# An attention pass whose VectorE turn is put in another order: products before differences, totals before the cap

## The reference, cut to what matters

```python
Q = _ln(h @ Wq[i], gq[i], bq[i])
K = _ln(h @ Wk[i], gk[i], bk[i])
qi = Q[src]
kj = K[dst]
score = (qi * kj).sum(-1) + 0.1 * (edge_attr * qi[:, :RBF]).sum(-1) + logm[dst]
smax = jax.ops.segment_max(score, src, num_segments=N)
es = jnp.exp(jnp.minimum(score - smax[src], 20.0))
denom = jax.ops.segment_sum(es, src, num_segments=N)
alpha = es / (denom[src] + 1e-10)
m = h[dst] @ Wm[i]
aggi = jax.ops.segment_sum(alpha[:, None] * m, src, num_segments=N)
```

## Time and profile before

| | |
|---|---|
| median of 3 runs | 11525.92 us (11525.92 to 11526.84) |
| the profiled execution | 11507.11 us, span 11505.3 us |
| busy in the span | PE 8060.2, PEld 6419.3, DVE 6381.7, ACT 3299.7, POOL 4649.4 us |
| the four attention passes | from 4787.25 to about 8521 us of the span, with tables and updates between them |
| `top` (L1648) | 1488 times, 683 ns each in the middle |
| `keys`, `products`, `totals` | 1488 times each, 358, 351 and 356 ns |
| `differences`, `capped` | 1488 times each, 158 and 156 ns |

### The profile page before, as it was taken

One profiled execution on the slowest core, in us unless ns is written; L12 is line 12 of the kernel. 1 busy time (PEld: TensorE's weight loads), 2 busy tenths in 40 slices (PEclk: granted clock), 3 DMA queues, 4 the chain that ended last, 5 costly groups with the idle time before them and its releaser, 6 DMA issues. The chain is left out here.

```text
span 11505.3 us, 328287 instructions
## 1 busy us (share of the span) xinstructions
PE 8060.2 (70%) x107650; PEld 6419.3 (56%) x107651; DVE 6381.7 (55%) x21371; ACT 3299.7 (29%) x11512; POOL 4649.4 (40%) x6184
## 2 busy tenths in 40 slices
PE   2999943234777588499599769949967889962323
PEld 1777732223555477499489659938963444443323
DVE  6444453335999767688678958868872010011112
ACT  3222211112333233266256536626640000010000
POOL 0777767775000166255145415514530000026665
PEclk9999985555767699799699879969988999955555
DMA  7222223334777699399279649928957889801112
GB/s 293 59 59 59 59 59 79 72 81 120 222 223 222 179 292 311 101 248 248 71 215 248 177 111 248 248 60 226 247 141 294 356 343 372 354 24 18 18 18 18
DMA packets 2228522, 1954.48 MB, mean 170 GB/s; under 512 B 1472897, under 2 KB 1871505, under 8 KB 2189698
## 3 DMA queue, kind: packets, MB, share of 16 engines
q1 hardware_dynamic: 1872642, 1712.86, 48.6%
q10 hardware_dynamic: 252000, 173.83, 4.9%
q0 software_dynamic: 103712, 65.58, 3.8%
HBM read 1478.99 MB, written 470.93 MB: 169 GB/s over the span
## 5 line engine op out<-in xcount | busy, mean ns | idle before, releaser
L1615 POOL TENSOR_TENSOR s_rest<-s_msg 128x196 f32<-128x196 f32 x1488 | 764.3, 514 | 2232.9 <-ACT s_msg L1597 1821.5
L2104 POOL DMA_INDIRECT l_row<-H,l_rec x816 | 786.9, 964 | 2158.9 <-DMA l_rec<-REC 1839.1
L1214 PE MATMUL s_gotd<-m_table_d,s_hot 128*128 x17856 | 1423.5, 205 | 201.1 <-DMA s_hot<-OHT 193.4
L1597 ACT ACTIVATE s_msg<-s_gotd,s_es 128x49 f32<-128x49 f32 x5952 | 1310.0, 304 | 48.7 <-ACT s_es L1590 0.5
L1214 PE MATMUL s_small<-m_table_s,s_hot 128*128 x17856 | 1301.6, 185 | 0.7 <-issue 0.2
L1214 PEld LDWEIGHTS s_gotd<-m_table_d,s_hot 128*128 128x128 bf16 x17856 | 1030.8, 96 | 399.0 <-issue 233.4
L846 DVE SCALAR_TENSOR_TENSOR a_acc<-a_acc,m_keep,a_sums 128x256 f32<-128x256 f32 x1488 | 707.2, 475 | 807.8 <-remote 751.6
L455 POOL DMA_INDIRECT REC<-rec,place x800 | 949.8, 1187 | 322.7 <-issue 215.1
L746 POOL DMA_INDIRECT REC<-m_meta,m_place x800 | 951.0, 1189 | 294.9 <-issue 243.6
L791 PE MATMUL a_ptr<-m_ident_bf,a_hd 128*128 128x128 bf16 x1488 | 295.0, 275 | 1094.3 <-DVE a_hd_weighted L832 756.0
L1648 DVE TENSOR_REDUCE s_tops<-s_mt 128x512 f32 (+1 forms) x1488 | 1014.7, 682 | 2.0 <-PE s_mt L1558 1.7
(11 more groups left out here) (414 smaller groups left out, 19900.6 us busy)
## 6 DMA issues: line engine op xcount, KB each, us to landing
s_hot<-OHT SPq DMA_DIRECT2D x1488, 384.0 KB
p_row<-ADJ SPq DMA_DIRECT2D x288, 1600.0 KB
ADJ<-a_acc SPq DMA_DIRECT2D x1488, 128.0 KB
s_rec<-REC SPq DMA_DIRECT2D x1488, 98.0 KB
OHT<-a_turned ACTq DMA_DIRECT2D x372, 384.0 KB
g_hot<-OHT SPq DMA_DIRECT2D x372, 384.0 KB
REC<-fill SPq DMA_DIRECT2D x124, 624.0 KB, 10.2
g_rec<-REC SPq DMA_DIRECT2D x372, 108.0 KB
```

The source lines that it names most:

```text
L1214: last = nc.tensor.matmul(out, hot, table[k][:, bass.ds(at, w)], start=(k == 0), stop=(k == 2))
L1597: last = nc.scalar.activation(msg[:, b % KEPT, j], gotd[b % KEPT][:, j, SW:2 * SW], ACT.Copy, scale=es[:, b % 2, j:j + 1])
L1615: nc.gpsimd.tensor_tensor(rest[:, b % KEPT].rearrange("p g w -> p (g w)"), msg[:, b % KEPT].rearrange("p g w -> p (g w)"), upper(msg[:, b ...
L2104: nc.gpsimd.indirect_dma_start(out=row[:, b, j], out_offset=None, in_=table, in_offset=bass.IndirectOffsetOnAxis(ap=rec[:, b, j, GIDX - NO ...
```

## The change

The list that orders VectorE's six stages in a turn is permuted; the stages, their lags, waits and increments stay the same.

```diff
-                laps(dve, [(keys, 1), (differences, 3), (products, 1), (capped, 3), (totals, 1), (top, 2)],
+                laps(dve, [(keys, 1), (products, 1), (differences, 3), (totals, 1), (capped, 3), (top, 2)],
                      SLOTS)
```

## The result

| | before | after |
|---|---|---|
| median, same chip | 11526.38 us (4 runs, 11525.92 to 11538.57) | 11600.47 us (4 runs, 11589.44 to 11619.53) |
| ratio | | 1.0063, interval 1.0046 to 1.0081 |
| the profiled execution | 11507.11 us | 11589.44 us, span 11587.6 us |
| four passes, first keys to last keys | 769.7, 769.9, 771.2, 772.0 us | 788.6, 788.8, 786.5, 788.6 us |
| a round of twelve turns, median | 23.90 us | 24.49 us |

The change makes the kernel slower by 74 us, 0.6%. The forecast was 11525 and its range ended at 11575. In the profiled executions 82 us came on; the four passes hold 69.7 of them between their first and last keys, and 116 rounds x 0.59 = 68 us of that. The rest had come on before the first pass (its first keys start at 4800.96 us of the span instead of 4787.25), in code that is the same.

A forecast was written before the change was run, and what follows sets the result against it. TensorE's own list, some 1.92 us a turn, was taken to bound the kernel. Floor cost 9 us minus branch gain 10 gave 11506 on the profiled 11507.1, plus 19 for timed runs: 11525; eight-in-ten range 11508 to 11575.

The forecast's parts named there:

- TensorE sets the regular turn at 1.92, neither wait holds it: Attention loop: TensorE works through its own list, some 1.92 us a turn, not held by its waits for differences or maximum.
- Products 0.39 behind keys, differences ending at 0.82: VectorE's regular turn: products move from 0.53 to 0.39 behind the keys' start, differences from 0.45 to 0.66, ending at 0.82.
- The order closes a loop that is a floor: Gathers' end, keys, products, differences, next gathers: a floor of 1.92 us a turn, costing 0.08 a round, 9 us.
- I take 0.05, being the row in which the wait itself is last.: Price of TensorE's wait for the differences at the gathers, 0.05 us, taken from a weight load in the adjacency pass.
- the bound of 0.13: Turn behind the branch: 0.13 us from differences' end to gathers holds the whole wait, so the floor is at most 2.00.
- the dearer wait: Rival, chance 0.14: the wait at the gathers costs more than 0.05; 11555 at a floor of 1.95, some 11604 at 2.00.
- The gain behind the branch: Turn behind the loop's branch: earlier maximum from totals ahead of the cap, turn from 2.01 to 1.92, 10 us gained.
- The caught cap: Rival, chance 0.16: the cap waits up to 0.37 for GpSimd's second subtraction; one hit a round 11546, three 11588.
- The prediction's 0.37: Turn behind the branch: the cap got through 0.37 us after the start of GpSimd's subtraction, of 0.51 recorded.
- No floor: Rival, chance 0.13: products start 0.27 behind keys like an unrelated neighbour, only a gain of 17 us remains, 11509.

The follow-up runs named there:

- Experiment 5: Kernel before, order unchanged, gathered maxima put in free columns of their own group's bank, gathers no longer wait for the differences; 10575.85 us against 10615.88, ratio 0.9965.
- experiment 1: Kernel before with only the products moved, directly behind the keys; cap still ahead of totals; 11495.52 us against 11406.79 for the kernel before, ratio 1.0086.
- experiment 6: Changed kernel with only the gathers' wait for the loaded data moved ahead of TensorE's address work; 10698.76 us against 10615.88 for the kernel before, ratio 1.0081.
- experiment 7: Changed kernel with the same three waits on the first gather, the differences' listed first; 10618.5 us against 10615.88 for the kernel before, ratio 1.0004.
- experiment 8: Changed kernel with the cap taken against a number in the instruction instead of a constant tile; 10689.78 us against 10615.88 for the kernel before, ratio 1.0072.
- Experiment 3: Changed kernel with gathered maxima in free columns of their group's bank, no gathers' wait for the differences; 11337.67 us against 11406.79 for the kernel before, ratio 0.994.
- experiment 4: Changed kernel with the gathers' waits for data and messages moved ahead of TensorE's address work; 11626.29 us against 11406.79 for the kernel before, ratio 1.0187.
- experiment 2: Kernel before with only the totals moved ahead of the cap; 11429.82 us against 11406.79 for the kernel before, ratio 1.0016.

## Why the prediction was wrong, step by step

- *TensorE sets the regular turn at 1.92, neither wait holds it.* Right. Experiment 5 takes the wait for the differences away in the old order and the rounds stay at 23.9.
- *Products 0.39 behind keys, differences ending at 0.82.* Right, 0.39 to 0.40 and 0.82. The view that gave it was one pair in another part of the pass.
- *The order closes a loop that is a floor.* Right, and it is what costs: in the changed kernel and in experiments 1, 6, 7 and 8 the regular turn is 0.82 (keys' start to differences' end) + the wait + 1.05, to within 0.01: 1.99 with a wait of 0.12 and 1.92 with one of 0.05. Experiment 3, without the wait, has the own pace again.
- ***"I take 0.05, being the row in which the wait itself is last."*** This step failed. The wait measured 0.11 to 0.12 in all regular turns looked at. The floor is 1.99, not 1.92, and a loop that stood exactly at TensorE's pace stands 0.07 above it: ten turns a round, 116 rounds. The earlier trace rows is a weight load that carries its one wait itself; the gathers' first load carries the first of three, and the differences' wait, the last, stands on an extra instruction ahead of it (experiment 7). That instruction, which makes the wait 0.06 dearer, is the term that the sum left out. It is in the kernel before as well, 1476 times at line 1545, so its view could have shown it beforehand. The prediction had the number of waits in view, as what spoke for a dearer one; experiments 6 and 7 show that the place in the list decides, not the number.
- *What the bound of 0.13 was worth.* As a bound it holds: the wait is no dearer than 0.13, and the range should have reached there. That it lies so near 0.12 is chance. In experiment 5, which has no such wait, the same turn behind the branch shows the same step:

```profile
4353.40 0.16 DVE L1654 TENSOR_TENSOR s_diff<-s_raw,s_gotd 128x4 f32<-128x4 f32 x1 [0.36 <-PE s_gotd L1565]
...
4353.70 0.17 PEld L1214 LDWEIGHTS s_gotd<-m_table_d,s_hot 128*128 128x128 bf16 x3
```

  0.14 from 4353.56, and 0.136 is the median of this step in every kernel but experiment 4 (0.156), whatever the wait. It is TensorE's own list between two kinds of work, as the 0.22 is in a regular turn.
- *The figure for the dearer wait.* The prediction has 11604 for a floor of 2.00, and 11600 came. The nearness is luck in part: the sum kept 8 us of gain behind the branch, where a floor of 2.00 leaves 0.01 of the 2.01, some 1 us, so 11612 is what its terms give. With the floor that came, 1.99, they give (0.75 - 9 x 0.01) x 116 - 2 = 74 us, 11600. So the mechanism and its other terms were right and one was mis-sized; the chance of 0.14 on the dearer wait was low, and the range ended before it.
- *Why a small error weighed so much.* Between 0.05 and 0.12 the loop crosses the pace of the engine that bounds the kernel. Below it the term costs nothing, above it every hundredth costs about 12 us (116 x 10 x 0.01).
- *The gain behind the branch.* There in the maximum (TensorE takes it 0.08 behind its last load instead of 0.23), and 0.22 in the turn from keys to keys, but by the gathers only 0.02 to 0.04 instead of the forecast 0.09, because its floor is 1.99 too. The cause given for it was wrong in part: with the totals moved alone (experiment 2) it doesn't come, and with the products moved alone (experiment 1) most of it does.
- *The caught cap.* It exists: of 1488 caps 22 were recorded for over 0.3 us in regular turns of the changed kernel, 7 before. One of them, in the timeline of the changed kernel:

```profile
5168.69 0.36 DVE L1635 SCALAR_TENSOR_TENSOR s_key<-s_rec,s_gotd 128x196 f32<-128x196 f32 x1 [0.18 <-PE s_small L1214]
...
5169.73 0.52 POOL L1622 TENSOR_TENSOR s_least<-s_rest 128x196 bf16<-128x196 f32 x1
5169.75 0.51 DVE L1660 TENSOR_TENSOR s_diff<-s_diff,m_cap 128x4 f32<-128x4 f32 x1
...
5170.78 0.34 DVE L1635 SCALAR_TENSOR_TENSOR s_key<-s_rec,s_gotd 128x196 f32<-128x196 f32 x1
```

  That turn takes 2.09 instead of 1.99. At 0.1 each, 22 of them are 2 us: a real mechanism, but one hit in some five rounds, not the one to three a round that its rival was priced at. Why so few were hit was not tested; in experiment 4, where turns of 1.94 and 2.24 alternate, over 400 caps outside the turn behind the branch were over 0.3 us. The prediction's 0.37 took the cap's usual 0.16 off its end. The rows show only the end, and it is the same in every long cap, 0.53 behind the subtraction's start, which is the subtraction's own end (0.51) and 0.02: nothing here shows that the cap got through before the subtraction was done.
- *No floor.* Refuted by every turn: products start 0.39 behind keys (median of all regular turns), while an instruction that waits for nothing starts 0.26 to 0.27 behind one of the same length.

What stays open: why the runs of the changed kernel spread over 30 us where those of before lie within 13.

## What to carry to other kernels

Before an order closes a loop through two engines, add up that loop and set it beside the pace of the bounding engine; when the two are within a tenth of a microsecond, price the forecast at both ends of the least certain term, and let the range reach the upper bound. A wait's price read at one instruction holds at another only if the wait sits on both in the same way: ask for the line of the wait and see whether it has an instruction of its own. When an instruction waits for several semaphores, write the wait that comes last in time first, and look in the trace where it landed: here three lines in another order gave back 0.06 us a turn, the whole loss. Better still, ask what the wait protects: a few columns in another bank removed it, and that kernel is the best of all that ran, 0.5 to 0.6% under before (11337.67 against 11406.79, 11351.77 against 11409.9).

## What the runs showed of the hardware

- The price of a wait that really holds TensorE, from the end of VectorE's instruction to the start of the weight load: 0.115 us listed last of three or of two, where it stands on an extra instruction of 0.051; 0.05 to 0.07 listed first of three, 0.05 to 0.08 alone, where the load carries it itself.
- A wait isn't free in code written out turn by turn even where the loop doesn't notice it: 24 turns took 77 to 78 us with it and 66 to 67 without, in both orders (about 45 us over four passes), because the address instructions of the gathers queue up behind it.
- The cap that reads one tile and a number was recorded for 0.40 us beside the subtraction behind the branch, the one that reads two tiles for 0.38; the long ones of both kinds end at the same place, 0.54 and 0.53 behind the subtraction's start. The Trainium skill (SBUF — State Buffer, Who interferes with whom) states that a VectorE instruction with at most one SBUF input and outside the two-port modes doesn't contend with GpSimd, and counts `tensor_scalar` among those that can enter such a mode. So 0.40 agrees with it only if this small instruction ran in one; no row here tells the mode. In regular turns with the number 9 caps were long instead of 22, so the form may matter there, but so few can also be chance.
